# A vision-transformer block on one core: attention folded by query position, second norms split over two engines, FFN order and outputs rearranged

## The chip, the cores and the metric

One core of one Trainium2 chip runs the whole program. The metric is the device time of one execution in microseconds (us); lower is better. The kernel before takes 272.5 us (median of 3 runs, 272.32 to 272.61). Engines are named as in the profile: PE is TensorE (PEld its weight loads), DVE is VectorE, ACT is ScalarE, POOL is GpSimd, SP is SyncE, which here only issues transfers.

## The reference, cut to what matters

32 images of 128x128 become 64 patch tokens each, plus one class token; the width is 128 channels. Then one attention layer and one layer of experts, each behind a layer norm:

```python
h = tok(x)                                     # (32, 64, 128), gated noisy linears, + positions
h = concat([cls_tok, h], axis=1)               # (32, 65, 128)
# attention, 8 heads of 16 channels, relative positions in keys and values
attn1 = einsum('bhqd,bhkd->bhqk', rq, rk)
attn2 = einsum('bhqd,qkd->bhqk', rq, rel_k[idx])
attn = softmax((attn1 + attn2) / sqrt(c), axis=-1)
w1 = einsum('bhqk,bhkd->bhqd', attn, rv)
w2 = einsum('bhqk,qkd->bhqd', attn, rel_v[idx])
h = h + (w1 + w2) @ Wo + bo                    # input: layernorm(h)
# experts on xf = layernorm(h)
probs = softmax(xf @ Wr.T + br); comb = the two largest of 8, the rest 0
o_e = gelu(xf @ W1[e] + b1[e]) @ W2[e] + b2[e]     # hidden width 256
h = h + sum_e comb[:, e] * o_e
```

## The kernel before, in words

Everything stays in SBUF in float32. The 2048 patch tokens are 16 tiles of 128 (one tile is a pair of images, 2 x 64 positions); the 32 class tokens are a 17th, small tile. Four tiles are a block of 512 tokens (`BLK`). Every engine runs a program of its own, written out by hand in order; `S[...]` are semaphores, so an instruction that waits holds all that stands behind it on its engine.

Stages: tokens and first norm (to about 45 us), relative-key scores (to 69 us), the loop over 16 pairs of images (to about 117 us), relative values, projection and second norm (to 148 us), experts (to the end).

The pair loop. PE turns scores (`turn_scores`, L1201), makes the next pair's (`scores`), turns probabilities (`turn_probs`, L1221) and multiplies them with values (`values`). DVE takes the maxima (L744, L751), writes the difference for the class key (L756), the reciprocal of the sum (L762), adds the relative scores for the next pair (`add`, L728), copies the turned probabilities out (`probs`, L769) and, every second pair, the products (`outputs`, L819). ACT does 8 exponentials of 64 columns per pair (L496). POOL scales the probabilities (L351). After the loop DVE spreads the class-key probabilities (`repeat`, L825), PE turns them (L1249), DVE multiplies and adds them (`class_key`, L836 and L841). Meanwhile POOL forms the low part of the first expert weights (`w1_lo`, L355), after ACT has made the high part.

Relative values: for each query position q one matrix of relative values goes against `PT` (the turned probabilities), 4 column groups per q, 256 matmuls, into banks 4 to 7 (`region_c,RVBD` in the rows). DVE adds them with the value bias (L883) to `OT`, which is laid out image by image. Only then does the projection with Wo run, its tiles again pairs of images. The residual is added by DVE for blocks 0 and 1 (L901), by PE through an identity product for blocks 2 and 3. Moments (L633, L636), the power -0.5 on POOL (L367), normalising on DVE (L648), turning on PE (`turn2`, L1325), two evacuations on ACT (L509, L510), and `low` (the part that the high-precision format leaves over; POOL for blocks 0, 1, DVE for the rest, L928) lead to the experts.

Experts: `up(e, blk)` is 6 matmuls of 416 columns (three products of high and low parts, twice), ACT's gelu follows (L518), `down(e, g)` multiplies with W2, DVE accumulates with the routing weight (L992). `up(0, *)` runs between the turns, then `up(1, *)`; two `down` groups of expert 0 come ahead of the routing weights' turn (L1401). At the end SP issues nine output transfers (L280, L283).

`keep_warm(n)` is n products of the identity whose result nobody reads.

## Time and profile before

| what | us |
|---|---|
| median of 3 runs | 272.5 |
| profiled execution, whole | 271.41 |
| its span (first to last instruction) | 269.6 |
| PE busy | 240.5 (89%) |
| DVE busy | 163.9 (61%) |
| ACT busy | 129.5 (48%) |
| POOL busy | 60.3 (22%) |

The granted clock of TensorE is 9 tenths or more in all 40 slices, 1.000 on average (its higher level, 2.4 GHz). A busy engine is not always the one that decides: the share is an average over stages. In the rows, times are from the start of the span; the bracket at the end of a row is the idle time before it and what ended it.

### The profile page before, as it was taken

The numbers are of one execution on the slowest core, as the hardware profiler recorded it, in microseconds if no ns is written. First come the engines' busy times: TensorE is split into PE (matmuls) and PEld (weight loads), VectorE is DVE, ScalarE is ACT, GpSimd is POOL, SyncE is SP. The second block draws the span as 40 slices with busy tenths as digits, with TensorE's granted clock in tenths as the row PEclk, the third lists the DMA queues.
The fourth block names the chain that finished last, engine by engine and source line by source line (L and its number), as shares of the span: only waits on it lengthen the run. The fifth ranks groups of instructions, "written<-read, shape, count | busy, mean of one in ns | idle before, by whom it ended". The sixth has DMA issues, their size and how long they took to land.

```text
span 269.6 us, 6432 instructions
## 1 busy us (share of the span) xinstructions
PE 240.5 (89%) x2519; PEld 206.7 (77%) x2519; DVE 163.9 (61%) x512; ACT 129.5 (48%) x432; POOL 60.3 (22%) x77
## 2 busy tenths in 40 slices
PE   0999997999896788897599989999999999999993
PEld 0855564898774565676479988899999999999993
DVE  0576898635579999999779655535252525252453
ACT  1543047942397999980004886440707071717100
POOL 8930122292013535365015300000000000000000
PEclk9999999999999999999999999999999999999999
DMA  6960000000000000090000000000000000000015
GB/s 214 284 151 2 1 0 0 2 4 0 2 0 4 2 2 2 25 291 5 2 5 0 0 4 0 2 0 2 0 0 1 2 0 2 0 4 0 0 29 131
DMA packets 6554, 7.95 MB, mean 29 GB/s; under 512 B 833, under 2 KB 5295, under 8 KB 6396
## 3 DMA queue, kind: packets, MB, share of 16 engines
q1 hardware_dynamic: 5260, 6.32, 8.3%
q10 hardware_dynamic: 720, 0.87, 1.2%
q8 instruction: 20, 0.33, 0.5%
q0 software_dynamic: 544, 0.35, 0.5%
q14 instruction: 10, 0.08, 0.1%
HBM read 6.47 MB, written 1.06 MB: 28 GB/s over the span
## 4 chain that ended last, share of the span: by engine, by line
PE 61%; DVE 24%; DMA 4%; issue 3%; ACT 3%; POOL 2%; SPq 1%; DVEq 0%
PE banks L1002 55%; DMA region_a<-in_x 4%; DVE stb L728 3%; DVE top L744 3%; DVE stb L648 2%; DVE stats L633 2%; DVE xnT L841 2%; PE banks L1201 2%; DVE region_c L769 2%; ACT region_d L518 2%; POOL rstd L317 2%; DVE mv L636 1%; DVE h L624 1%; DVE ntop L751 1%; SPq L259 1%
## 5 line engine op out<-in xcount | busy, mean ns | idle before, releaser
L992 DVE SCALAR_TENSOR_TENSOR KT<-banks,vbd,KT 128x128 f32<-128x128 f32 (+1 forms) x136 | 38.1, 343 | 59.1 <-PE banks L1002 59.1
L518 ACT ACTIVATE region_d<-banks,vecs 128x416 f32<-128x416 f32 x80 | 45.5, 612 | 47.7 <-PE banks L1002 47.6
L1002 PE MATMUL banks<-w_all,region_d 128*128 128x128 f32 (+1 forms) x544 | 63.3, 276 | 0.0
L1002 PEld LDWEIGHTS banks<-w_all,region_d 128*128 128x128 f32 (+1 forms) x544 | 61.3, 187 | 1.6 <-issue 0.5
L496 ACT ACTIVATE region_e<-banks,ntop 128x64 f32<-128x64 f32 x128 | 38.2, 325 | 6.9 <-DVE rsum L762 3.5
L1002 PE MATMUL banks<-x_hi,w_hi 128*128 128x416 f32 x80 | 29.7, 371 | 1.3 <-ACT region_d L518 1.3
L1002 PE MATMUL banks<-x_lo,w_hi 128*128 128x416 f32 x80 | 28.2, 353 | 0.0
L1002 PE MATMUL banks<-x_hi,w_lo 128*128 128x416 f32 x80 | 28.2, 352 | 0.0
L496 ACT ACTIVATION_READ_ACCUMULATOR region_e<-banks,ntop 128x1 f32 x128 | 27.8, 217 | 0.0
L351 POOL TENSOR_TENSOR region_e<-region_e,rsum 128x512 f32<-128x512 f32 (+1 forms) x16 | 16.5, 1030 | 37.3 <-DVE rsum L762 37.3
L1002 PEld LDWEIGHTS banks<-x_hi,w_hi 128*128 128x128 f32 x80 | 15.1, 189 | 3.5 <-ACT region_d L518 2.0
L1201 PE MATMUL banks<-kc,stb 128*128 128x128 f32 x64 | 10.3, 284 | 7.6 <-DVE stb L728 7.6
L1002 PE MATMUL banks<-kc 128*128 128x128 f32 x70 | 10.2, 292 | 6.6 <-DMA kc<-in_consts 6.6
L1002 PE MATMUL banks<-region_d,relk_bd 64*128 64x64 f32 x256 | 15.3, 288 | 0.0
L1002 PEld LDWEIGHTS banks<-x_lo,w_hi 128*128 128x128 f32 x80 | 15.0, 188 | 0.2
L1002 PEld LDWEIGHTS banks<-x_hi,w_lo 128*128 128x128 f32 x80 | 15.0, 188 | 0.2
L1002 PEld LDWEIGHTS banks<-region_d,relk_bd 64*128 64x128 f32 x256 | 14.6, 188 | 0.6 <-issue 0.5
L1002 PE MATMUL banks<-region_b,wnT 128*128 128x512 f32 x32 | 14.7, 598 | 0.2 <-DVE region_b L566 0.2
L1201 PEld LDWEIGHTS banks<-kc,stb 128*128 128x128 f32 x64 | 6.8, 141 | 9.9 <-DVE stb L728 9.9
L1002 PEld LDWEIGHTS banks<-kc 128*128 128x128 f32 x70 | 9.0, 202 | 6.8 <-DMA kc<-in_consts 6.6
L1002 PE MATMUL banks<-region_c,RVBD 128*32 128x32 f32 x520 | 9.3, 240 | 5.0 <-issue 3.7
L1002 PEld LDWEIGHTS banks<-region_c,RVBD 128*32 128x32 f32 x520 | 8.3, 127 | 5.7 <-issue 4.2
(219 smaller groups left out, 379.3 us busy)
## 6 DMA issues: line engine op xcount, KB each, us to landing
region_a<-in_x SPq DMA_DIRECT2D x2, 512.0 KB, 6.3
region_a<-in_x SPq DMA_DIRECT2D x1, 1024.0 KB, 10.3
w_sb<-in_L_ffn_W SPq DMA_DIRECT2D x1, 1024.0 KB, 5.9
out<-KT SPq DMA_DIRECT2D x8, 128.0 KB, 2.4
region_d<-in_L_attn_rel_v SPq DMA_DIRECT2D x2, 260.0 KB, 9.2
kc<-in_consts ACTq DMA_DIRECT2D x1, 336.0 KB, 5.8
region_d<-in_L_tok_eps_in ACTq DMA_DIRECT2D x2, 128.0 KB, 7.5
region_d<-in_L_tok_W_w ACTq DMA_DIRECT2D x1, 128.0 KB, 7.2
```

What stands on the lines that cost most here:

```text
L317: g.tensor_tensor(rstd[:, n * TPB:(n + 1) * TPB], ve[:, n * TPB:(n + 1) * TPB], mhalf[:, :], ALU.pow).then_inc(S["rstd_ok"], 1)
L351: g.tensor_tensor(ev, ev, rv, ALU.mult).then_inc(S["pn_ok"], 1)
L496: last = a.activation(dst[:, h // 2, h % 2], src[:, h // 2, h % 2], ACT.Exp, scale=SCALE, bias=ntop[:, o + h:o + h + 1], accum_out=esum[:, ...
L518: a.activation(HB[:, e % 2, s, blk * FB:(blk + 1) * FB], bank[h_bank(i)][:, 0:FB], ACT.Gelu, bias=vecs[:, v:v + 1]).then_inc(S["gelu_ok"], 1)
L633: last = v.bn_stats(stats[0:m, 6 * t:6 * t + 6], src[0:m, t * C:(t + 1) * C])
L648: last = v.tensor_scalar(ST[n % 2][0:m, i * C:(i + 1) * C], src[0:m, t * C:(t + 1) * C], mv[0:m, 2 * t:2 * t + 1], rstd[0:m, t:t + 1], ALU ...
L728: v.tensor_tensor(ST[p % 2].rearrange("p (g j m) -> p g j m", g=2, j=2), banks[:, 0:1024].rearrange("p (g h j m) -> p g h j m", g=2, h=2, ...
L744: most = mark(v.tensor_reduce(top[:, o].rearrange("p (j s) -> p j s", j=PJ), bank[2 + p % 2][:, :].rearrange("p (j k s) -> p j s k", j=PJ, ...
L769: v.tensor_copy(PT[:, :, 2 * p:2 * p + 2, 0:NPATCH], bank[4 + p % 2][:, :].rearrange("p (j b q) -> p j b q", j=PJ, b=2)).then_inc(S["pt_ok ...
L992: last = v.scalar_tensor_tensor(acc[0:m, t, :], bank[out_bank(u)][0:m, i * C:(i + 1) * C], comb[0:m, t, e:e + 1], acc[0:m, t, :], op0=ALU. ...
L1002: return t_.matmul(o, l, r, start=start, stop=stop)
L1201: last = t_.transpose(bank[2 + p % 2][:, j * P:(j + 1) * P], ST[p % 2][:, j * P:(j + 1) * P], ident)
```

## The change

The parts, in the order of the program:

1. Class scores (`class_products`) are computed as four 32-row groups instead of full 128-row products padded with zeros.
2. In the loop, POOL writes the class-key difference (`difference`) and spreads the class-key probabilities (`repeat`), two pairs at a time; PE turns them in the loop (`turn_pc`), DVE multiplies them in the loop (`class_key`, 256 columns), and `outputs` adds them and the value bias while it copies.
3. `OT` is laid out by query position: column = 32 q + image. A tile of 128 columns is now four query positions of 32 images. So a block of 16 positions can be projected once its relative values are there. The residual `h0` must have the same layout: SP writes it to the output tensor in HBM in the old layout and reads it back in the new one, during the loop.
4. The relative values are cut into halves of a block, with the projections and the first turn between them, and one identity product (`keep_warm(1)`) behind every four positions of the first six quarters.
5. The residual is DVE's in all four blocks; the second norm of blocks 0 to 2 is ACT's (`norm2`, with a factor and an offset `nmr` = -mean x rstd that DVE and POOL prepare), of the rest DVE's; `low` is DVE's throughout.
6. `up(0, blk)` and `up(1, blk)` alternate; gelu number i belongs to `UNITS[i]`. Four `down` groups of expert 0 (`AHEAD = 4`, before 2) come ahead of the routing weights' turn.
7. The last expert takes the class tile first and tiles 12 to 15 in two halves (`LAST`); the outputs are issued by SP and ACT.

```diff
+LAST = [range(16, 17), range(0, 4), range(4, 8), range(8, 12), range(12, 14), range(14, 16)]
+AHEAD = 4
-OP_BANKS = (5, 6, 2, 3)
+OP_BANKS = (1, 2, 3, 5)
+REL_BANKS = (4, 5, 6, 0)
+        OTq = OT[:, :].rearrange("p (q b) -> p q b", b=IMG)
+        UNITS = [(e, blk, s) for blk in range(5) for e in range(2) for s in range(2)]
+        UNITS += [(e, blk, s) for e in range(2, E) for blk in range(5) for s in range(2)]
...
 # SP, during the pair loop
+            sp_.wait_ge(S["h0o_ok"], 1)
+            sp_.wait_ge(S["st_ok"], 5)
+            for b2 in range(2):
+                sp_.dma_start(ov[b2, 1:QC, :, :], h0v[64 * b2:64 * b2 + 64, :, :]).then_inc(S["d_h0s"], 16)
+            sp_.wait_ge(S["d_h0s"], 32)
+            sp_.wait_ge(S["st_ok"], 10)
+            for f in range(4):
+                sp_.dma_start(h0v[32 * f:32 * f + 32, :, :], oq[f]).then_inc(S["d_h0q"], 16)
...
 # POOL, pair loop
+            for p in range(PAIRS + 2):
+                if p < PAIRS:
+                    difference(p)
+                if p >= 2:
+                    normalised(p - 2)
+                    if p % 2 == 1:
+                        repeat((p - 3) // 2)
...
 # ACT
-            for n in (2, 3):
-                act.wait_ge(S["op_ps"], n + 1)
-                a.activation(KT[:, n * BLK:(n + 1) * BLK], bank[OP_BANKS[n]][:, :], ACT.Copy).then_inc(S["h1a_ok"], 1)
+            def norm2(n):
+                act.wait_ge(S["nmr_ok"], n + 1)
...
+                    last = a.activation(ST[n % 2][0:m, i * C:(i + 1) * C], KT[0:m, t * C:(t + 1) * C], ACT.Identity,
+                                        bias=nmr[0:m, t:t + 1], scale=rstd[0:m, t:t + 1])
...
 # DVE, pair loop: outputs and class key
-                v.tensor_copy(OT[:, 256 * u:256 * u + 256].rearrange("p (b q) -> p b q", b=4), o[:, :, 0:NPATCH])
+                dve.wait_ge(S["pcx_ok"], u + 1)
+                v.scalar_tensor_tensor(OTq[:, :, 4 * u:4 * u + 4].rearrange("p q b -> p b q"), o[:, :, 0:NPATCH],
+                                       vecs[:, V_BV:V_BV + 1], own(u), op0=ALU.add, op1=ALU.add)
...
 # DVE, behind the loop
+            attended(0)
+            attended(1)
+            residual(0)
+            attended(2)
+            residual(1)
+            attended(3)
+            low(0)
+            attended_class()
+            residual(2)
+            low(1)
+            residual(3)
...
+            low(2)
+            norm2(3)
+            norm2(4)
...
 # PE, behind the loop
-            for n in range(1, 5):
-                turn2(n)
-                router(n - 1)
...
-                up(0, n - 1)
+            filled(0, range(16))
+            filled(1, early)
+            project(0)
+            relative(1, late)
+            relative(2, early)
+            project(1)
+            relative(2, late)
+            relative(3, early)
+            project(2)
+            turn2(0)
+            relative(3, late)
+            relative_class()
...
+            project(3)
...
+            up(0, 0)
+            turn2(1)
+            router(0)
+            up(1, 0)
+            up(0, 1)
+            turn2(2)
...
```

How the rows move, at three places. First DVE in the pair loop, an odd pair from its maxima on; before:

```order
L744 TENSOR_REDUCE top<-banks 128x8
L751 SCALAR_TENSOR_TENSOR ntop<-top,nSc 128x8
L756 TENSOR_TENSOR region_e<-ntop,nSc 128x8
L762 RECIPROCAL rsum<-esum 128x8
L728 TENSOR_TENSOR stb<-banks,region_a 128x512
L769 COPY region_c<-banks 128x4x2x64
L819 COPY xnT<-banks 128x256
L820 COPY OTc<-banks 128x4
L740 TENSOR_TENSOR esum<-esum,region_e 128x8
```

and the same stretch after (`xnT` is the memory of `OT`, `region_c` that of `PT`):

```order
L824 TENSOR_REDUCE top<-banks 128x8
L832 SCALAR_TENSOR_TENSOR ntop<-top,nSc 128x8
L838 RECIPROCAL rsum<-esum 128x8
L914 TENSOR_TENSOR tmpx<-banks,vcq 128x256
L808 TENSOR_TENSOR stb<-banks,region_a 128x512
L849 COPY region_c<-banks 128x4x2x64
L900 SCALAR_TENSOR_TENSOR xnT<-banks,vecs,tmpx 128x4x64
L902 COPY OTc<-banks 128x4
L820 TENSOR_TENSOR esum<-esum,region_e 128x8
```

The small difference (L756) has left DVE, the class-key product (L914) has come in, and the copy has become an addition.

Second, PE from the last values on (`RVBD` relative values, `wqkvo` the projection, `kc` alone a fill, `stb` a turned norm); before:

```order
L1002 MATMUL banks<-region_c,vbd 32x65 x8
L1002 MATMUL banks<-region_c,RVBD 32x32 x256
L1002 MATMUL banks<-p0x,kc 128x32
L1002 MATMUL banks<-region_c,RVBD 32x32 x4
L1002 MATMUL banks<-h,kc 128x512
L1002 MATMUL banks<-wqkvo,xnT 128x128 x8
L1002 MATMUL banks<-wqkvo,OTc 32x128
L1002 MATMUL banks<-wqkvo,xnT 128x128 x4
L1002 MATMUL banks<-h,kc 128x512
L1002 MATMUL banks<-wqkvo,xnT 128x128 x4
L1002 MATMUL banks<-kc 128x128 x9
L1325 MATMUL banks<-kc,stb 128x128 x4
```

and after, from the sixth quarter of the relative values on:

```order
L1075 MATMUL banks<-region_c,RVBD 32x32 x16
L1075 MATMUL banks<-kc 128x128
L1075 MATMUL banks<-wqkvo,xnT 128x128 x4
L1075 MATMUL banks<-region_c,RVBD 32x32 x64
L1075 MATMUL banks<-wqkvo,xnT 128x128 x4
L1075 MATMUL banks<-region_c,RVBD 32x32 x64
L1075 MATMUL banks<-wqkvo,xnT 128x128 x4
L1396 MATMUL banks<-kc,stb 128x128 x4
L1075 MATMUL banks<-region_c,RVBD 32x32 x32
L1075 MATMUL banks<-p0x,kc 128x32
L1075 MATMUL banks<-region_c,RVBD 32x32 x4
L1075 MATMUL banks<-kc 128x128 x2
```

Three of four projections and the first turn now stand between the relative values, and the two products with `h` are gone.

Third, DVE behind the loop; before:

```order
L883 SCALAR_TENSOR_TENSOR xnT<-banks,vecs,xnT 128x32x16 x4
L886 SCALAR_TENSOR_TENSOR OTc<-banks,vecs,OTc 128x32
L888 SCALAR_TENSOR_TENSOR OTc<-banks,clsv,OTc 128x32
L891 TENSOR_TENSOR clsr<-clsr,bob 32x128
L892 MEMSET lg 128x8
L893 MEMSET vbd 128x640
L901 TENSOR_TENSOR KT<-banks,h 128x512
L633 BN_STATS stats<-KT 128x6 x4
L636 BN_AGGR mv<-stats 128x2 x4
L638 TENSOR_SCALAR ve<-mv 128x4
```

and after:

```order
L945 TENSOR_TENSOR xnT<-banks,xnT 128x512 x2
L960 TENSOR_TENSOR KT<-banks,h 128x512
L710 BN_STATS stats<-KT 128x6 x4
L713 BN_AGGR mv<-stats 128x2 x4
L717 TENSOR_SCALAR nmr<-mv 128x4
L719 TENSOR_SCALAR ve<-mv 128x4
L945 TENSOR_TENSOR xnT<-banks,xnT 128x512
L960 TENSOR_TENSOR KT<-banks,h 128x512
```

The first residual stands behind two blocks of relative values instead of four, and the next blocks follow in turns.

## Rows read from the trace of the kernel before

**Rows 1.** Busy time by stretch: length, engines (busy, count), clock, DMA share, GB/s.

```profile
core 0: us, PE busy (x) PEld busy (x) DVE busy (x) ACT busy (x) POOL busy (x), PEclk, DMA share, GB/s
121.80:136.30 14.50, 9.49 (x536) 8.59 (x525) 11.30 (x15) 0.00 (x0) 3.38 (x1) 1.00 0.02 5
136.30:147.80 11.50, 11.17 (x91) 9.72 (x84) 10.56 (x54) 2.90 (x6) 4.33 (x4) 1.00 0.01 1
147.80:165.30 17.50, 16.20 (x98) 14.93 (x98) 10.60 (x36) 15.11 (x29) 2.92 (x3) 1.00 0.01 1
165.30:265.30 100.00, 99.99 (x764) 95.66 (x762) 39.93 (x138) 36.51 (x65) 0.00 (x0) 1.00 0.03 6
```

**Rows 2.** Timeline of PE: start, length, instruction; idle time before it in brackets.

```profile
113.97 1.38 PE L1002 MATMUL banks<-kc 128*128 128x128 f32 x10
...
122.85 2.14 PE L1002 MATMUL banks<-region_c,RVBD 128*32 128x32 f32 x128 [0.46 <-issue]
126.30 1.77 PE L1002 MATMUL banks<-region_c,RVBD 128*32 128x32 f32 x103 [1.31 <-issue]
...
134.03 1.77 PE L1002 MATMUL banks<-region_c,RVBD 128*32 128x32 f32 x103 [1.58 <-issue]
...
137.27 1.95 PE L1002 MATMUL banks<-wqkvo,xnT 128*128 128x128 f32 x16
...
146.51 0.63 PE L1325 MATMUL banks<-kc,stb 128*128 128x128 f32 x4 [0.33 <-DVE stb L648]
...
147.80 0.46 PE L1002 MATMUL banks<-x_hi,w_hi 128*128 128x416 f32 x1
```

**Rows 3.** Timeline of DVE, one even and one odd pair of the loop.

```profile
90.47 0.67 DVE L728 TENSOR_TENSOR stb<-banks,region_a 128x512 f32<-128x512 f32 x1
...
92.62 0.17 DVE L751 SCALAR_TENSOR_TENSOR ntop<-top,nSc 128x8 f32<-128x8 f32 x1
92.82 0.17 DVE L756 TENSOR_TENSOR region_e<-ntop,nSc 128x8 f32<-128x8 f32 x1
92.91 0.20 DVE L762 RECIPROCAL rsum<-esum 128x8 f32<-128x8 f32 x1
93.02 0.67 DVE L728 TENSOR_TENSOR stb<-banks,region_a 128x512 f32<-128x512 f32 x1
...
95.79 0.67 DVE L728 TENSOR_TENSOR stb<-banks,region_a 128x512 f32<-128x512 f32 x1
```

**Rows 4.** The page's costliest groups, two of ACT: busy, mean ns, idle, releaser.

```profile
L518 ACT ACTIVATE region_d<-banks,vecs 128x416 f32<-128x416 f32 x80 | 45.5, 612 | 47.7 <-PE banks L1002 47.6
...
L496 ACT ACTIVATE region_e<-banks,ntop 128x64 f32<-128x64 f32 x128 | 38.2, 325 | 6.9 <-DVE rsum L762 3.5
```

**Rows 5.** Timeline of PE at the loop's start, class scores.

```profile
71.91 1.60 PE L1002 MATMUL banks<-KT,wnT 128*128 128x128 f32 x12
```

**Rows 6.** Timeline of DVE behind the loop.

```profile
120.69 0.68 DVE L836 TENSOR_TENSOR tmpx<-banks,vcq 128x512 f32<-128x512 f32 x1
121.40 4.32 DVE L841 TENSOR_TENSOR xnT<-xnT,tmpx 128x512 f32<-128x512 f32 x1
...
138.46 0.69 DVE L901 TENSOR_TENSOR KT<-banks,h 128x512 f32<-128x512 f32 x1 [0.29 <-PE banks L1002]
...
141.49 0.87 DVE L633 BATCH_NORM_STATS2 stats<-KT 128x6 f32<-128x128 f32 x4
142.40 0.38 DVE L636 BATCH_NORM_AGGREGATE mv<-stats 128x2 f32<-128x6 f32 x4
```

**Rows 7.** Timeline of POOL behind the loop.

```profile
120.39 4.79 POOL L355 TENSOR_TENSOR w_lo<-w_sb,w_hi 128x2048 fp32r<-128x2048 f32 x1 [1.33 <-ACT w_hi L504]
...
143.06 1.04 POOL L367 TENSOR_TENSOR rstd<-ve,mhalf 128x4 f32<-128x4 f32 x1 [1.28 <-DVE ve L638]
```

**Rows 8.** Timeline of SP at the end.

```profile
267.23 0.61 SPq L283 DMA_DIRECT2D out<-KT  x1
```

**Rows 9.** The page's DMA issues: KB each, us from issue to landing.

```profile
out<-KT SPq DMA_DIRECT2D x8, 128.0 KB, 2.4
...
out<-KT SPq DMA_DIRECT2D x1, 16.0 KB, 2.0
```

433 lines of the change are left out of this document (236 added, 197 removed).

## The prediction

> **What bounds the kernel now.** I read the busy time by stretch first. From 165.3 to 265.3 us PE is busy 99.99 of 100 us, and from 147.8 to 165.3 it works 16.20 of 17.50 [rows 1]: the experts are PE's own work, and a change of order saves there at most the 1.3 us of gaps. Between 121.8 and 136.3 PE is busy 9.49 of 14.50 us, and from 136.3 to 147.8 it seems busy (11.17 of 11.50), but only until the first `up` at 147.80 [rows 1, 2], with 15 `keep_warm` products and two identity products of the residual among the rest. So of the 26 us between the last values (121.8) and the first `up` much is waiting or fill. The timeline of PE shows what kind: after every 128 product records (64 matmuls) of relative values it stops "on issue", 1.31 and 1.58 us; two blocks of 128 records start 126.30 - 122.85 = 3.45 us apart, and another pair 1.58 + 2.14 = 3.72 apart, while the work is 2.14 [rows 2]. It looks as if the code itself arrives at such a rate: 128 records each 3.45 to 3.72 us. The second wait is DVE's: L841 stands 4.32 us where another 512-column addition (L901) takes 0.69, and it ends soon after POOL's `w1_lo` (120.39 + 4.79 = 125.18) [rows 6, 7]. And residual, moments, power, normalising and turning follow one another only after all relative values. In the pair loop DVE is the pace: 2.55 us for an even pair, 2.77 for an odd one (starts of L728) [rows 3]; ACT is idle only 6.9 us in the whole loop [rows 4].
>
> **The change part by part.** Times below are those of the profiled execution (span 269.6, whole 271.41); the median of the runs is 272.5, 1.1 above it, and I add this again at the end.
>
> Class scores. 12 records take 1.60 us [rows 5] for 6 products, three such portions; in four column groups 32 rows each run side by side, so 16 products of 32 rows should take half. PE then no longer holds DVE in the first three pairs. Bounds: 0 (DVE's and ACT's own work hides it) and 2.4 us (three portions shortened by half of 1.60); DVE's and ACT's work lies close behind PE's there, so I take 1.0 gained, somewhat under the middle.
>
> The loop. DVE loses L756: from L751 to L762 pass 0.29 us now, 0.1 of them needed, so 0.2 is saved per pair [rows 3]. An odd pair gains `class_key`, 256 columns: between the 0.17 of an 8-column and the 0.67 of a 512-column operation [rows 3], 0.42 long, some 0.35 to the next start. `outputs` has two more operands but the same 256 columns: 0. Two pairs: 5.32 - 0.4 + 0.35 = 5.27 against 5.32; ACT's floor is below (it idles 6.9 us in 16 pairs [rows 4]). So per pair nothing changes. Bounds over 8 double pairs: -1.6 (if the copy hid anyway) and +2.4 (if DVE waits 0.3 us per double pair for the two turns that PE now makes in front of the scores). I take 0. POOL gets the difference, and a copy of 256 columns every second pair, some 0.5 to 0.9 us each; its share of the loop is under half now, so that is hidden; what it costs without cover is the rival D below.
>
> Behind the loop. The four 512-column copies of DVE (`repeat`) and six of its eight class-key operations, among them the one of 4.32 us, are no longer there. But PE still runs 5 + 3 fills (1.38 us for 5 [rows 2]), the last turns wait for ACT's last pair and POOL, and DVE has the last class key between. Followed, the last values end at about 119.8 instead of 121.8: 2.0 earlier (1.0 from the start of the loop, 1.0 here). Bounds 0.5 and 3.5.
>
> From the relative values to the first `up`. PE's work in the new order: 256 matmuls, 4 x 2.14 = 8.6; four projections at half of 1.95 = 3.8; 8 fills at 0.27 = 2.2; one turn 0.5, the class row and its projection 0.9. Sum 15.9 to 16.0. Records: 512 + 32 + 16 + 16 = 576, that is 4.5 blocks of 128. At 3.72 per block the code needs 16.7, at 3.45 15.5; but blocks whose own work is longer (projections in them) don't lend time to others. Block by block the excess is 0.8, 0.4, 0.75, 0.35 at 3.72, sum 2.3; at 3.45 it is 1.3. I take 2.3, and 0.3 for small waits on data: 18.5. The first `up` starts at 119.8 + 18.5 = 138.3 instead of 147.8: 9.5 earlier.
>
> Do data arrive in that time? DVE: relative block 1 is complete on PE at about 128.0, `attended(1)` 0.7, then residual 0.69, moments 0.87 + 0.1 + 0.38, two small ones, to 131.0 [rows 6]; POOL's power 1.04 [rows 7] and a small product to 132.5; ACT's four of 128 columns, each between the 0.325 of 64 and the 0.612 of 416 columns [rows 4], about 1.1, to 133.8. PE wants the first turn at about 133.8 as well: a draw, so a wait here is likely to be small, and each later one similarly: `low(0)` ends at 137.2, before `up(0, 0)`. Queued behind `residual(0)` on DVE is `attended(2)` (project(2) waits for it), behind each `norm2` on ACT the gelus and evacuations. From the first `up` PE has about 3.9 us per block (two `up`, one turn, one router), and per block DVE needs 2.3 + 0.7, ACT 1.1 + 1.2 + 2.4 = 4.7 at first, later less, since DVE norms the last blocks: ACT is the tight one, but PE runs some banks ahead. I cost that at 0, bounds 0 and 4.
>
> Experts. `turn2(1)` and `router(0)` were ahead of the first `up` and are now behind it: 147.80 - 146.51 = +1.3 [rows 2]. The gaps of 1.3 us between 147.8 and 165.3 [rows 1] should go: four `down` groups (7 us of PE work) now stand between the router and the turn of the routing weights, while the two table loads and DVE's selection run; by hand comb is ready at 160.4 and PE comes to its turn at 163.2. So -1.3. Bounds: -1.3 and +1.5.
>
> The end. 4.3 us pass from PE's last product to the end (265.3 to the span of 269.6) [rows 1]: DVE's accumulation, SP's last issue at 267.23, 2.0 us landing [rows 8, 9]. After: two tiles instead of four plus one in DVE's last turn (saves some 0.5), but two issues of 0.61 in each queue behind one another and 2.4 for the larger ones [rows 8, 9]. I take 0; bounds -1.0 and +0.5.
>
> HBM round trip of `h0`: eight quarter-megabytes in and out during the loop, where the queues are empty; it is wanted at about 128.7 and issued before 96. It has more than 30 us for 16 times what lands in 2.4 [rows 9]. Cost 0; without that cover the first residual would wait for it.
>
> Sum: -9.5 + 1.3 - 1.3 + 0 = -9.5. Profiled execution 271.4 - 9.5 = 261.9; median 272.5 - 9.5 = 263.0.
>
> **Two rules weighed.** On code: the trace shows the stops of 1.31 and 1.58 us per 128 records [rows 2]. The Trainium skill, "Runtime: NRT & Kernel Launch", section "Instruction fetch mechanics", says that code comes in blocks of 256 instructions and that crossing a block's edge is mostly hidden. A block of 256 is 128 products with their weight loads, so the spacing agrees; "mostly hidden" does not here. By the page the stretch would take 2.3 less, 260.7 in all.
>
> B, the hand-overs hold PE: ACT (norm, two evacuations, gelus) or the in-order DVE queue is late at turns 0 to 3. For it speaks the draw at 133.8 and ACT's 4.7 against 3.9 per block; against it, that PE has banks to run ahead. Price: 0.8 per block for four blocks and a first turn 1 us late, +4: 267.
> C, it goes better: fills cover the code stops (2.3) or the loop ends earlier: 260.5. For it: a fill takes only 2 records for 0.27 us, so blocks are longer; against it: they still fall short of 3.72.
> D, slower: one mechanism, DVE's two-SBUF operations in the loop (L740, L751) waiting behind POOL's longer turn. If each pair met one whole POOL operation (1.04, the size of the power operation in [rows 7]; L351 is as long), 14 pairs cost 14.6: 263.0 + 14.6 = 277.6. It decides from 9.5 / 14 = 0.68 us a pair. Against it: POOL's turn begins with the reciprocal and DVE's next two operations read PSUM, so that only the end of the spreading copy can meet L740, some 0.2 us.
> E, nothing of the early `up` remains because the projection by query position needs all relative values anyway (it doesn't do what it says): 272. Against it: the tile's columns are four positions of all images, and its wait is for one block.
>
> **How the numbers follow.** A 0.55 (its own range 261 to 265.5), B 0.24, C 0.16, D 0.03, E 0.02. The range 259.5 to 268 leaves out the far part of C, and of B, and D and E, together under 0.2. Within 0.2% (0.5 us) is about what a measurement of this kernel can tell from no change. Faster 0.95, same 0.02, slower 0.03.
>
> **What would show it.** Right: the first 416-column product at about 138, turn 0 waiting under 1 us, PE without a gap over 0.5 from there to its end at about 256, no DVE operation of 4 us, L914 in 0.42 and double pairs of 5.3. Wrong: PE waiting for `stb` or for x_lo by more than 1 us per block (B), `issue` stops gone (C), L820 or L832 over 0.5 us in the loop (D), project(0) waiting for the last relative block (E). Should the granted clock fall from its higher level (2.4 GHz, all stretches of [rows 1] show it) in the new order, all sums of PE are off.

## The result and the profile after

The changed kernel takes 261.57 us (median of 4 runs, 260.73 to 262.57), the kernel before beside it 272.41 (272.25 to 272.61): ratio 0.960, 95% interval 0.956 to 0.964, faster. The forecast was 263.0. The profiled execution took 261.36 us, 10.1 less than the 271.41 of before; its span is 259.5.

The page's busy time and clock. PE is busy 91% of a shorter span, and no slice has a granted clock under 0.9 of full speed, that is the higher level, 2.4 GHz:

```profile
PE 236.2 (91%) x2507; PEld 202.2 (78%) x2507; DVE 153.7 (59%) x485; ACT 132.5 (51%) x442; POOL 64.4 (25%) x104
...
PEclk9999999999999999999999999999999999999999
```

Busy time by stretch, against [rows 1]:

```profile
120.00:137.00 17.00, 16.43 (x581) 14.05 (x578) 8.42 (x32) 3.25 (x8) 6.94 (x5) 1.00 0.03 6
137.00:155.00 18.00, 18.00 (x116) 16.43 (x116) 11.57 (x45) 15.79 (x32) 3.23 (x4) 1.00 0.00 1
155.00:255.00 100.00, 100.00 (x765) 96.31 (x765) 43.50 (x152) 39.05 (x69) 0.00 (x0) 1.00 0.02 6
```

From 120 to 137 PE works 16.43 of 17.00 us, where it worked 9.49 of 14.50 in the stretch of the relative values before; from 137 on it has no gap. The timeline of PE there, against [rows 2]:

```profile
120.13 0.66 PE L1075 MATMUL banks<-region_c,RVBD 128*32 128x32 f32 x32
120.72 0.49 PE L1075 MATMUL banks<-kc 128*128 128x128 f32 x2
121.14 0.67 PE L1075 MATMUL banks<-region_c,RVBD 128*32 128x32 f32 x32
...
126.14 1.06 PE L1075 MATMUL banks<-wqkvo,xnT 128*128 128x128 f32 x8
127.13 2.15 PE L1075 MATMUL banks<-region_c,RVBD 128*32 128x32 f32 x128
...
131.73 1.39 PE L1075 MATMUL banks<-region_c,RVBD 128*32 128x32 f32 x76 [0.42 <-issue]
...
134.36 0.66 PE L1396 MATMUL banks<-kc,stb 128*128 128x128 f32 x4
...
138.47 0.46 PE L1075 MATMUL banks<-x_hi,w_hi 128*128 128x416 f32 x1
```

The last values end and relative values begin at 120.13 (121.80 before); the first `up` starts at 138.47 (147.80). Projections (`wqkvo`) and the turn of block 0 (L1396) lie between relative values, and one stop on issue is left, 0.42 us, where there were 0.46, 1.31 and 1.58 [rows 2]. A group of 32 records comes every 1.02 us with its fill (120.13, 121.14), and 128 without fills take 2.15, so 32 take 0.54: a fill costs 0.48.

The chain that feeds the turn, on DVE, POOL and ACT. DVE's operation of 4.32 us [rows 6] is gone:

```profile
128.35 0.69 DVE L945 TENSOR_TENSOR xnT<-banks,xnT 128x512 f32<-128x512 f32 x1 [3.68 <-PE banks L1075]
128.96 0.68 DVE L960 TENSOR_TENSOR KT<-banks,h 128x512 f32<-128x512 f32 x1
...
131.32 1.02 POOL L411 TENSOR_TENSOR rstd<-ve,mhalf 128x4 f32<-128x4 f32 x1 [6.83 <-DVE ve L719]
...
132.66 1.65 ACT L574 ACTIVATE stb<-KT,nmr,rstd 128x128 f32<-128x128 f32 x4 [12.80 <-POOL nmr L415]
```

The chain starts when PE ends block 1 of the relative values (L945 waits for it). It ends at 134.31, and PE takes the turn at 134.36. The draw that the prediction saw at 133.8 looks like one here; the run below tells which side ends last.

One double pair of the loop on DVE, against [rows 3]; from one L808 to the next but one is 97.79 - 92.36 = 5.43 us (5.32 before):

```profile
92.04 0.40 DVE L914 TENSOR_TENSOR tmpx<-banks,vcq 128x256 f32<-128x256 f32 x1
92.36 0.68 DVE L808 TENSOR_TENSOR stb<-banks,region_a 128x512 f32<-128x512 f32 x1
...
93.55 0.65 DVE L900 SCALAR_TENSOR_TENSOR xnT<-banks,vecs,tmpx 128x256 f32<-128x256 f32 x1
94.05 0.16 DVE L902 COPY OTc<-banks 128x4 f32<-128x4 f32 x1
...
94.89 0.17 DVE L832 SCALAR_TENSOR_TENSOR ntop<-top,nSc 128x8 f32<-128x8 f32 x1
94.98 0.20 DVE L838 RECIPROCAL rsum<-esum 128x8 f32<-128x8 f32 x1
...
97.79 0.68 DVE L808 TENSOR_TENSOR stb<-banks,region_a 128x512 f32<-128x512 f32 x1
```

The experts: the routing weights (L1036) are there at 159.46, and PE comes to their turn (L1507) at 163.11 without idling:

```profile
159.16 0.30 DVE L1036 TENSOR_TENSOR vbd<-rt 128x136 f32<-128x136 f32 x1
...
163.11 0.60 PE L1507 MATMUL banks<-kc,vbd 128*128 128x128 f32 x4
```

The end, against [rows 8]; the last product ends at 249.80 + 5.86 = 255.66 us, 3.84 before the span does:

```profile
249.80 5.86 PE L1075 MATMUL banks<-w_all,region_d 128*128 128x128 f32 x51
...
251.50 6.27 SPq L304 DMA_DIRECT2D out<-KT  x10
251.50 6.37 ACTq L614 DMA_DIRECT2D out<-KT  x10
```

**A ruler for all runs.** The pair loop's first maximum (L824, L744 before) starts anywhere from 71.5 to 72.9 us in these executions. So each profiled execution is cut at that start, the first relative value, the first 416-column `up` and the last product's end, all read off the timelines:

| kernel | loop | relative values to first `up` | `up` to PE's end | tail | median, us |
|---|---|---|---|---|---|
| before | 50.28 | 26.00 | 117.49 | 4.31 | 272.4 |
| after | 48.08 | 18.34 | 117.19 | 3.84 | 261.6 |
| after_again | 48.72 | 18.34 | 117.19 | 3.89 | 262.1 |
| e1_relative_first | 48.09 | 25.25 | 117.95 | 3.88 | 269.9 |
| e2_no_fills | 48.08 | 17.80 | 117.19 | 3.93 | 261.3 |
| e3_two_ahead | 48.04 | 18.36 | 117.71 | 3.86 | 262.1 |
| e4_one_queue | 48.07 | 18.34 | 117.18 | 6.87 | 265.0 |
| e5_dve_norms | 48.06 | 19.11 | 118.04 | 3.96 | 263.5 |
| e6_no_loop_fills | 48.07 | 19.73 | 117.18 | 3.87 | 262.9 |
| e7_rows_of_four | 48.67 | 18.34 | 117.19 | 3.87 | 262.8 |
| e8_dc_on_dve | 51.54 | 18.36 | 117.16 | 3.90 | 265.3 |
| e10_contiguous | 47.56 | 18.35 | 117.18 | 3.92 | 260.8 |
| e12_both | 48.04 | 16.81 | 117.20 | 10.55 | 267.2 |
| e13_images_first | 47.56 | 17.16 | 117.17 | 3.92 | 260.3 |

Where an edit doesn't touch a stretch, it repeats to 0.05 us nearly everywhere (the tail to 0.12), so an edit is read from its own stretch far better than from the medians, whose intervals are about 0.3 to 0.5% (0.8 to 1.3 us). The loop of after_again is an outlier; the granted clock was 0.89 from 69 to 84 us, around its start (1.00 in the first profile). So the 10.1 us are: loop -2.20, relative stretch -7.66, experts -0.30, tail -0.47, and +0.53 for a later start of the loop in that execution. The stretches of before and after don't hold quite the same work: before, the turn and the routing product of the next block (146.51 to 147.80, 1.3 us [rows 2]) stand ahead of the first `up`; after, they stand behind it. Like for like the relative stretch is about 6.4 shorter and the experts about 1.6.

### The profile page after: what moved, and what is told of

It is laid out like the page before. It is cut to its first block, busy times and chain, and to the rows that moved or that the text cites. A ratio compares the mean times of both kernels' runs of the same rounds, so it can differ in the third digit from the quotient of the medians.

```text
span 259.5 us, 6469 instructions
## 1 busy us (share of the span) xinstructions
PE 236.2 (91%) x2507; PEld 202.2 (78%) x2507; DVE 153.7 (59%) x485; ACT 132.5 (51%) x442; POOL 64.4 (25%) x104
## 3 DMA queue, kind: packets, MB, share of 16 engines
q10 hardware_dynamic: 1952, 1.41, 1.9%
## 4 chain that ended last, share of the span: by engine, by line
PE 63%; DVE 17%; issue 6%; ACT 4%; POOL 4%; DMA 4%; ACTq 1%; DVEq 0%; POOLq 0%
PE banks L1075 58%; DMA region_d<-in_L_tok_W_sw 4%; DVE top L824 4%; DVE stb L808 3%; POOL w_lo L405 2%; ACT region_e L541 2%; PE banks L1276 2%; POOL rstd L338 2%; DVE stb L728 2%; DVE region_c L849 2%; DVE stats L710 1%; DVE h L701 1%; PE banks L1396 1%; ACT w_hi L549 1%; PE banks L1085 1%
## 5 line engine op out<-in xcount | busy, mean ns | idle before, releaser
L541 ACT ACTIVATION_READ_ACCUMULATOR region_e<-banks,ntop 128x1 f32 x128 | 31.8, 255 | 0.0
L1075 PE MATMUL banks<-region_d,relk_bd 64*128 64x64 f32 x256 | 15.3, 288 | 0.0
L1075 PEld LDWEIGHTS banks<-kc 128*128 128x128 f32 x56 | 8.0, 208 | 7.4 <-DMA kc<-in_consts 6.5
L824 DVE TENSOR_REDUCE top<-banks 128x8 f32<-128x512 f32 x16 | 11.0, 687 | 1.9 <-PE banks L1276 1.4
L1075 PE MATMUL banks<-region_d,region_b 64*128 64x128 f32 x128 | 11.4, 297 | 0.3 <-ACT region_a L517 0.3
```

Source lines behind the costliest of these rows:

```text
L541: last = a.activation(dst[:, h // 2, h % 2], src[:, h // 2, h % 2], ACT.Exp, scale=SCALE, bias=ntop[:, o + h:o + h + 1], accum_out=esum[:, ...
L824: most = mark(v.tensor_reduce(top[:, o].rearrange("p (j s) -> p j s", j=PJ), bank[2 + p % 2][:, :].rearrange("p (j k s) -> p j s k", j=PJ, ...
L1075: return t_.matmul(o, l, r, start=start, stop=stop)
```

## The experiments

**after_again**, the changed kernel once more.

> The changed kernel itself, as the mark for the three runs beside it, which differ from it by less than 1 us each. Expected: 261.6 us, within 0.3% of its own first result, and the same marks in the trace within 0.1 us: last values ended about 120.1, first 416-column up product at 138.5, last product at 255.7.

262.07 us (ratio 0.961, 0.956 to 0.966). Its marks lie 0.65 us later, all from the loop, and here the draw at turn 0 went the other way:

```profile
135.00 0.66 PE L1396 MATMUL banks<-kc,stb 128*128 128x128 f32 x4 [0.67 <-ACT stb L574]
```

PE waits 0.67 us for ACT, but it had no stop on issue ahead of that, and the stretch is 18.34 us again. The turn comes 14.22 us after the first relative value here and 14.23 in the first profile. So do those of e3, e4, e7 and e10 (14.23 or 14.24), where PE waits 0.51 to 0.84 us for ACT. What ends last at turn 0 is therefore the chain over DVE, POOL and ACT, in the first profile too; its stop of 0.42 us on issue cost nothing.

**e1_relative_first**, the order alone.

```diff
             filled(1, early)
-            project(0)
             relative(1, late)
-            relative(2, early)
-            project(1)
-            relative(2, late)
-            relative(3, early)
-            project(2)
-            turn2(0)
-            relative(3, late)
+            relative(2, range(16))
+            relative(3, range(16))
+            pe.wait_ge(S["o_ok"], 1)
             relative_class()
+            project(0)
+            project(1)
+            project(2)
+            turn2(0)
```

> Edit: TensorE's order behind the loop. The changed kernel runs the projections 0 to 2 and the turn of block 0 between the relative values of the next positions; here all 512 records of relative values and the class ones come first, then projections 0, 1, 2 and the turn; fills, layout and all the rest stay. Theory: the gain of 9.3 us ahead of the first up product comes from this order, since the chain from a projection to its turned block (residual, norm, POOL's power, ScalarE, turn: 5.2 us from 128.96 to 134.36 by VectorE's L960 to L1396) then runs beside relative values. Without it the projection of block 0 comes at about 134.5 instead of 126.1, its residual at 137.4, turn 0 at 142.8, and the first up product, behind block 0's evacuations and its neighbours' columns, at about 144 to 146: 267 to 268 us, +6 us against the changed kernel. Rival: the order only fills gaps in the delivery of TensorE's code (the run without the six fills showed that 6 x 0.48 us of fills hid in it, all but 0.5 us of it), so that the records take as long and the later chain costs 2 us or less: 264. Either way the relative stretch itself would show issue stops again between 127 and 134, because nothing lies between the records there: 3 blocks of 128 records at 3.1 to 3.9 us.

269.93 us (ratio 0.990, 0.987 to 0.993); the stretch is 25.25 us, 6.9 longer, nearly the 26.00 of before. Without the interleaving the stretch is 0.75 us under that of before, which holds 1.3 us more work; the order brings the rest. (The wait on `o_ok` keeps the class values out of a bank that DVE still reads; it is met by then.) The timeline of PE:

```profile
131.65 2.13 PE L1075 MATMUL banks<-region_c,RVBD 128*32 128x32 f32 x124 [1.30 <-issue]
...
135.10 0.30 PE L1075 MATMUL banks<-region_c,RVBD 128*32 128x32 f32 x6 [0.77 <-issue]
135.33 2.05 PE L1075 MATMUL banks<-wqkvo,xnT 128*128 128x128 f32 x16
139.53 1.16 PE L1075 MATMUL banks<-wqkvo,xnT 128*128 128x128 f32 x8 [2.15 <-DVE xnT L945]
142.00 1.11 PE L1396 MATMUL banks<-kc,stb 128*128 128x128 f32 x4 [1.31 <-ACT stb L574]
...
143.76 1.92 PE L1075 MATMUL banks<-wqkvo,xnT 128*128 128x128 f32 x8
```

and its busy time with the granted clock (0.51) just behind:

```profile
142.00:148.00 6.00, 6.00 (x24) 5.34 (x24) 3.45 (x15) 2.99 (x7) 1.21 (x3) 0.51 0.00 0
```

The expected stops come back, PE waits 3.46 us for data, and then something that I had not expected: behind these waits the granted clock is at its lower level (1.2 GHz), and the turn takes 1.11 us instead of 0.66, eight projection records 1.92 instead of 1.06. From the turn to the first `up` pass 4.17 us, where the same products take 2.45 in the changed kernel (134.36 to 134.94 and 136.60 to 138.47); so an estimate from these rows puts 1.7 of the 6.9 us down to the clock. The first `up` came at 146.17, just past the 144 to 146 expected.

**e2_no_fills**.

```diff
                 for i in range(part[0], part[-1] + 1, 4):
                     relative(n, range(i, i + 4))
-                    keep_warm(1, spare=3)
```

> Edit: the six 128-column filling products between the first six groups of relative values are taken out; nothing else. Theory of the fills: in the changed kernel a group of 32 records with its fill takes 1.02 us and 32 records of an unfilled run take 0.54 us (128 in 2.15), so a fill costs 0.48 us, not the 0.27 that I forecast; six are 2.9 us, and without them TensorE is at the first projection 2.9 us earlier. The first up product would then come up to 2.9 us earlier (135.6) unless VectorE's chain from the values to the residuals or the gelu side is late, which I expect to eat about half: total 260.0 (-1.5 us against the changed kernel). Rival, the code: the kernel before delivered 128 of these records per 3.72 us with 'issue' stops of 1.3 to 1.6 us; 192 unfilled records in a row would need 5.6 us, only 0.5 us less than the 6.1 us that they take with fills, the stops come back in the chain or the timeline, and the time is within 0.5 us of the changed kernel's. A third outcome, slower by over 1 us, would mean that the fills hold TensorE's granted clock up: then the clock of the stretch 120 to 137 would fall below 0.9.

261.28 us (ratio 0.957, 0.952 to 0.962). The stretch is 0.54 us shorter, for 2.9 us of work less:

```profile
120.98 2.39 PE L1075 MATMUL banks<-region_c,RVBD 128*32 128x32 f32 x144
124.09 0.91 PE L1075 MATMUL banks<-region_c,RVBD 128*32 128x32 f32 x48 [0.72 <-issue]
...
127.99 1.04 PE L1075 MATMUL banks<-region_c,RVBD 128*32 128x32 f32 x56 [0.67 <-issue]
...
131.99 1.17 PE L1075 MATMUL banks<-region_c,RVBD 128*32 128x32 f32 x64 [0.78 <-issue]
...
135.99 0.42 PE L1075 MATMUL banks<-region_c,RVBD 128*32 128x32 f32 x12 [0.36 <-issue]
```

2.53 us of stops come back. The records behind them start at 124.09, 127.99, 131.99 and 135.99, and between two of these starts there are each time exactly 128 records (48 + 72, 56 + 64 and 64 + 52 relative ones, the rest a projection or a projection and a turn): a block of code every 3.9 to 4.0 us. The rival holds: most of the fills stood where PE would have waited for its code. The clock stayed at 1.00. How much comes back is not the same in every execution, and the profiled one is the slowest of six (259.10 to 261.75 us). e12 and e13, further down, have the same order of products without fills, and their blocks arrive sooner: e13's start 3.62 and 3.73 us apart (122.83, 126.45, 130.18), and e12 passes two of them in 7.08 us.

The rows of e13:

```profile
122.83 0.91 PE L1077 MATMUL banks<-region_c,RVBD 128*32 128x32 f32 x48 [0.91 <-issue]
...
126.45 1.04 PE L1077 MATMUL banks<-region_c,RVBD 128*32 128x32 f32 x56 [0.41 <-issue]
```

So their stretches are 17.16 (e13) and 16.81 us (e12), and the fills are worth 0.5 to 1.5 us. Why the blocks arrive at different rates is open.

**e6_no_loop_fills**.

```diff
-                if PAIRS <= p < PAIRS + 2:
-                    if p == PAIRS:
-                        pe.wait_ge(S["pcx_ok"], 5)
-                    keep_warm(5 if p == PAIRS else 3, spare=0)
```

> Edit: the two blocks of filling products (five and three) that TensorE runs in the last two steps of the attention loop are taken out. In the changed kernel they lie at 113.72 (1.38 us) and 115.99 (0.94 us), ahead of the transposes of the last probabilities (115.03 and 116.76), and VectorE's last product waits for the second one until 117.18. Theory: they lie on the path, the last values end 0.5 to 0.8 us earlier (119.4 instead of 120.1), and so do the first up product and the end: 261.0. Rival: ScalarE's last exponentials (end 116.6) are what ends last there, TensorE just waits for them: 0.0 to -0.2 us. Second rival: TensorE's granted clock falls behind the loop without them (below 0.9 in 118 to 130), and the kernel is slower by 1 us or more.

262.93 us (ratio 0.964, 0.960 to 0.968), and nothing that I expected came as a whole:

```profile
115.83 0.66 PE L1298 MATMUL banks<-kc,region_e 128*128 128x128 f32 x4 [1.24 <-POOL region_e L384]
...
120.92 0.67 PE L1075 MATMUL banks<-region_c,RVBD 128*32 128x32 f32 x32
123.01 0.38 PE L1075 MATMUL banks<-kc 128*128 128x128 f32 x2 [1.41 <-issue]
```

In the fills' place PE waits for POOL's normalised probabilities, and the loop keeps its 48.07 us: the first rival was right that the fills cost nothing there, though it is POOL that ends last and not ACT. But a stop of 1.41 us appears behind the first 32 records of relative values, and the stretch grows by 1.39: the stop lies ahead of the chain to turn 0, where PE waits 0.81 us for ACT as well. Products taken out at one place moved a stop to another, where nothing covered it; whether by shifting the blocks' edges or by the time that PE gave the delivery, no run separates.

**e7_rows_of_four** and **e10_contiguous**, the mis-sized term. e10 leaves out the order of positions, so it isn't a replacement for the changed kernel. L900 writes with a stride (after), in runs of four with strided reads (e7), or contiguously (e10):

```diff
-  v.scalar_tensor_tensor(OTq[:, :, 4 * u:4 * u + 4].rearrange("p q b -> p b q"), o[:, :, 0:NPATCH],
-                         vecs[:, V_BV:V_BV + 1], own(u), op0=ALU.add, op1=ALU.add)
+e7  v.scalar_tensor_tensor(OTq[:, :, 4 * u:4 * u + 4], o[:, :, 0:NPATCH].rearrange("p b q -> p q b"),
+                           vecs[:, V_BV:V_BV + 1], own(u).rearrange("p b q -> p q b"), op0=..., op1=...)
+e10 v.scalar_tensor_tensor(OT[:, 256 * u:256 * u + 256].rearrange("p (b q) -> p b q", b=4),
+                           o[:, :, 0:NPATCH], vecs[:, V_BV:V_BV + 1], own(u), op0=..., op1=...)
```

> Edit: VectorE's addition of the own values (one 256-column scalar_tensor_tensor in each second pair of the loop) writes its result position by position, in contiguous runs of four elements, and reads PSUM and the own values with the stride instead; the same elements, the same place. In the changed kernel the operation is 0.65 us long and holds VectorE for 0.50 us to its next start; the same operation with contiguous writes took 0.33 before. Theory: the strided write is the 0.16 us per double pair that I had costed at nothing; turned to runs of four it goes back to 0.33 to 0.40, a double pair from 5.43 to 5.30, the loop ends 0.8 to 1.3 us earlier and so does the kernel: 260.5. Rival: a stride costs the same on either side (read or write), the operation stays at 0.50 and the time does not move (within 0.2 us); or it is worse, since two inputs are strided now: +0.1 us per double pair, +0.8 us.

> Edit: the 256-column addition of the own values writes its result contiguously, image by image, as the copy that it replaced did (L819 before: 0.41 us, 0.33 us to the next start). The output projection then reads the positions in another order than the rest of the kernel keeps them in, so the tokens of the result are permuted against the reference; no time hangs on the values. In the changed kernel it is 0.66 us with a strided write and was 0.65 us with strided reads instead. Theory: any stride beyond one element costs, on either side; contiguous, the operation falls to 0.42 us, a double pair from 5.43 to 5.27, the loop ends 1.2 us earlier: 260.6. Rival: it is the operation itself that is dear (three inputs: PSUM, a per-partition scalar and the own values), it stays at 0.65 us, and the time is that of the changed kernel. That would put my mis-sized term on the added operand and not on the new order of positions.

262.77 us (ratio 0.965) and 260.84 us (0.957, 0.954 to 0.960). L900 in the groups of e7 and of e10 (busy, mean ns, idle):

```profile
L900 DVE SCALAR_TENSOR_TENSOR xnT<-banks,vecs,tmpx 128x256 f32<-128x256 f32 x5 | 3.2, 649 | 0.0
```

```profile
L900 DVE SCALAR_TENSOR_TENSOR xnT<-banks,vecs,tmpx 128x256 f32<-128x256 f32 x4 | 1.9, 475 | 0.0
```

About 655 ns with strided writes, 649 with strided reads, 475 contiguous; the plain copy before took 414. Of the 0.24 us that the operation grew, 0.18 belong to the stride, on whichever side, and 0.06 to the two added operands. The loop became 0.52 us shorter, under half of what I expected, since a double pair fell by only 0.10 (5.34). What counts is the time to DVE's next start: 0.33 us for the copy (94.21 to 94.54), 0.50 after (93.55 to 94.05), 0.39 in e10 (94.27 to 94.66). The stride has 0.11 of these 0.17 us. In e7 it is 0.57 (94.32 to 94.89) at the same length, and a double pair is 5.51 (93.13 to 98.64): eight times 0.08 are the 0.6 us by which e7's loop is longer. The Trainium skill, "SBUF — State Buffer", section "Door 1: The DMA port swizzle", says that each access that crosses to a new 16-byte line of SBUF pays a penalty. The trace agrees in kind: strides of 128 bytes on the write (after) and of 256 on the SBUF read (e7) cost 0.18 us here, and runs of four elements on the write side did not help, since the reads then stride.

**e8_dc_on_dve**.

```diff
-                        dve.wait_ge(S["dc_ok"], p - 1)
+                    dve.wait_ge(S["top_ok"], p + 1)
+                    if p >= 4:
+                        dve.wait_ge(S["pc_ok"], p - 3)
+                    v.tensor_tensor(SP[p % 4][:, 512:520], ntop[:, o], nSc[:, p * H:(p + 1) * H], ALU.subtract)
```

> Edit: the subtraction that gives the class-key difference of a pair (128x8) goes from POOL back to VectorE, where the kernel before had it (its L756), right behind ntop; 16 of them. Theory: in the kernel before it took VectorE 0.09 us to the next start (92.82 to 92.91) and waited for ntop; VectorE is busy in all of the loop, so a double pair goes from 5.43 to 5.6 us and the loop ends 1.4 us later: 263.2. My prediction had counted 0.18 us a double pair for this move. Rival: POOL's hand-over (0.20 us of POOL, then ScalarE's exponentials behind it) is shorter when VectorE does it itself, ScalarE starts a pair earlier, and nothing is lost: 261.8, within 0.3 us. If POOL's shared path with VectorE mattered, VectorE's short operations L820 and L832 (0.15 and 0.17 us now) would get shorter without it; I expect them unchanged.

265.31 us (ratio 0.972, 0.969 to 0.976), more than either expectation. The expectation misstates the prediction's term, which was 0.4 a double pair, and that is what the timeline shows: 0.28 us from L829 to L840 against 0.09 from L832 to L838.

```profile
93.68 0.17 DVE L829 SCALAR_TENSOR_TENSOR ntop<-top,nSc 128x8 f32<-128x8 f32 x1
93.88 0.17 DVE L834 TENSOR_TENSOR region_e<-ntop,nSc 128x8 f32<-128x8 f32 x1
93.96 0.20 DVE L840 RECIPROCAL rsum<-esum 128x8 f32<-128x8 f32 x1
```

The loop is 3.46 us longer, and 16 x 0.19 = 3.0 of it is this. So this small move carries more than the whole gain of the loop: without it the loop would be 1.3 us longer than before.

**e3_two_ahead**: `AHEAD = 2`, with `down(0, 2)` and `down(0, 3)` behind the first `base`.

> Edit: two groups of down products ahead of TensorE's turn of the routing weights instead of four (the number that bounds the buffer goes from 4 to 2, the two others follow behind base(0)). In the changed kernel the routing weights (comb) are ready at 159.46 and TensorE comes to them at 163.11. Two down groups are about 2 x 1.55 us of TensorE, so it would come at about 160.0, still 0.5 us behind their being ready. Theory, as I now read the trace: +0.0 to +0.5 us. My prediction put 1.3 us on this edit of the change (gaps ahead of the routing weights that go); if that holds, the time is 1.3 us longer and an idle time ahead of L1507 shows. Rival: with fewer groups ahead, ScalarE's gelus of the next blocks fall behind TensorE and up products wait for buffers: more than +1.5 us.

262.07 us (ratio 0.961, 0.958 to 0.964). The stretch from the first `up` is 0.52 us longer: the upper end of what I expected, under half of the prediction's 1.3. The turn of the routing weights (L1504) comes at 160.44, right behind DVE's last step of the selection (L1036, 160.00 to 160.30), where the changed kernel leaves 3.65 us between:

```profile
160.44 0.63 PE L1504 MATMUL banks<-kc,vbd 128*128 128x128 f32 x4
```

**e4_one_queue**: ScalarE's ten block transfers and the class row's go to SyncE.

> Edit: all 21 output transfers are issued by SyncE's queue; ScalarE's queue issues none. In the changed kernel each queue issues half, 0.43 to 0.45 us each, and the execution ends 3.84 us behind the last product. The last group (tiles 14 and 15) has four transfers: in one queue its fourth is issued 2 x 0.43 us later. Theory: the tail is 0.9 us longer (4.7 us), +0.3% in all, with 262.5 us against 261.6; if the earlier groups' issues are not done by the time the last values come, a little more, up to +1.7. Rival: the landing of the transfers, not their issue, ends the execution, and the tail is unchanged within 0.2 us.

265.04 us (ratio 0.973, 0.970 to 0.975): a tail of 6.87 us, 3.0 longer, three times my figure.

```profile
252.27 9.47 SPq L306 DMA_DIRECT2D out<-KT  x20
```

All twenty issues of the blocks stand in one row from 252.27 to 261.74. The first of them starts 4.16 us before PE's end (256.43), and in that time one queue issues nine at 0.47. I had counted only the last group.

**e5_dve_norms**: second norm of blocks 0 to 2 by DVE.

> Edit: the second norm of blocks 0 to 2 goes from ScalarE (four activations, 1.65 us, behind a product of mean and deviation on VectorE and POOL) to VectorE, as blocks 3 and 4 have it in the changed kernel; only the power stays on POOL. In the first two profiles of the changed kernel turn 0 started at 134.36 (no wait) and 135.00 (0.67 us wait for ScalarE's L574): data and TensorE arrive within 0.7 us of each other. Theory: VectorE does a block's norm in about 1.2 to 1.7 us plus the hand-over, but it has in hand the next residual (0.68) and its statistics, so turn 0 moves by -0.3 to +0.5, and the turns 1 to 3 come later because VectorE (11.6 us busy of the 18 from 137 on) gets about 4 us more work there. TensorE's up products wait for x_lo by 0.5 to 2 us: 262.5 to 263.5. Rival: VectorE has room, the norms hide, and what ScalarE saves (4.95 us) brings the gelus and nothing else forward: within 0.3 us of the changed kernel.

263.50 us (ratio 0.967, 0.965 to 0.970), at the far end of the expected range: 0.77 us in the relative stretch and 0.85 behind it. The row of PE at the class row's projection:

```profile
139.66 0.41 PE L1068 MATMUL banks<-wqkvo,OTc 128*32 128x128 f32 x2 [1.35 <-DVE OTc L942]
```

The norms' price is what queues behind them on DVE: here the class row, for whose projection PE waits, and behind it on PE the first `up`.

**e12_both**: e2, the last group split in two, and one transfer per tile.

```diff
-                for f in range(2):
-                    sp_.dma_start(oq[f][:, tt, :], acc[32 * f:32 * f + 32, tt, :])
+                for t in (t for t in tiles if t % 2 == 0):
+                    sp_.dma_start(ot[t], acc[:, t, :])      # ot: "b (t f) c -> t f b c"
```

> A version meant to beat both. Edits: the six fills between the first relative values taken out (0.5 to 0.8 us in their own run); one output transfer per token tile of all 128 partitions, even tiles by SyncE and odd ones by ScalarE, 17 issues of 64 KB in place of 21 of 32 or 64 KB; and the last expert's last group of two tiles split in two of one tile. Expected: behind the last value there is one VectorE operation (0.28) instead of two, one issue per queue (0.45) instead of two, then the landing (1.8 us): tail 3.84 to 3.1 us; with the fills' 0.5 the time is 260.4 us, -1.2 against the changed kernel. Rival: a transfer that reads 128 partitions of 512 bytes is no quicker to land than two of 32 partitions and two tiles, or the landing grows with the issues in flight (e4: one queue, tail 6.9 us): tail unchanged, 261.2.

267.19 us (ratio 0.981, 0.977 to 0.984): a tail of 10.55 us, 6.6 longer instead of 0.7 shorter. The DMA share (tenths) and GB/s in 40 slices of 250 to 266, first e12, then the changed kernel in 250 to 260:

```profile
DMA  0000122222222222222222222222222222220000
GB/s 0 0 0 0 23 79 74 84 76 82 77 87 79 87 85 86 81 82 78 86 87 87 87 85 87 86 87 86 87 87 86 86 86 87 86 77 4 0 0 0
```

```profile
DMA  2000000004899800489980028999945647200000
GB/s 60 2 0 4 0 0 0 0 0 96 150 312 230 250 12 0 92 141 314 236 250 16 0 63 150 285 250 299 250 125 152 158 105 185 78 0 0 0 0 0
```

The transfers run at 86 GB/s with a share of 0.2 to 0.3, a quarter of the sixteen engines, against up to 314 GB/s and nine tenths. The Trainium skill, "DMA: Bandwidth & Descriptors", section "Why a DMA increments its semaphore by 16 and not by 1", has the number of engines chosen by the outermost dimension of both patterns; mine was 4 in HBM, 32 in the changed kernel, and the trace agrees. The issues also changed in number and partitions, and no run changed this dimension alone. Its relative stretch (16.81) has the order of e2, with two stops (1.11 and 0.51 us) for e2's four.

**e13_images_first**: e2's edit; L900 contiguous; the position order made behind the loop by the four additions.

```diff
-                o = OT[:, n * BLK:(n + 1) * BLK]
-                v.tensor_tensor(o, bank[REL_BANKS[n]][:, :], o, ALU.add)
+                v.tensor_tensor(OTp[:, n * BLK:(n + 1) * BLK].rearrange("p (q b) -> p q b", b=IMG),
+                                bank[REL_BANKS[n]][:, :].rearrange("p (q b) -> p q b", b=IMG),
+                                OTq[:, 16 * n:16 * n + 16, :], ALU.add)
```

> A version meant to beat both, with the full result. Edits: the six fills between the first relative values are taken out, and the order of positions is no longer made in the loop: VectorE's addition of the own values writes contiguously, image by image (0.475 us in the run of the contiguous write, against 0.655), and the four 512-column additions of the relative values behind the loop (L945) read the attended values with the stride and write the position order into the free place of the probabilities, from which the projection reads. Expected from the two single runs: the loop 0.5 us shorter (a double pair 5.43 to 5.335), the fills 0.5 to 1.5 us, together 260.3 us, -1.5 against the changed kernel (pooled 261.8). The four additions have a strided input now; two inputs at 512 columns already take 0.69 us, so I expect 0.69 to 1.05 each, and 0.4 us at most of it ahead of turn 0, hidden behind relative values: 0. Rival: turn 0 is already the last to come without fills (TensorE there at 133.3 to 134.1), the stride costs 0.36 us on the chain to it, and half of the gain goes again: 261.0. Second rival: VectorE's stride by 64 elements collides with something and the additions take 2 us: slower than 262.

260.33 us (ratio 0.957, 0.954 to 0.960), the best version: loop -0.52, relative stretch -1.18 against the changed kernel's first profile. The additions take 1.03 to 1.06 us instead of 0.69, hidden as expected:

```profile
125.99 1.06 DVE L945 TENSOR_TENSOR region_e<-banks,xnT 128x512 f32<-128x512 f32 x1 [3.14 <-PE banks L1077]
```

The changed kernel's medians are 261.57 and 262.07, so this is 1.2 to 1.7 less, but the ratios' intervals overlap (0.954 to 0.960 against 0.956 to 0.964). The loop's -0.52 is as in e10. Of the -1.18, e2's and e12's 17.80 and 16.81 tell that up to 1 us depends on how fast the code arrived in the execution.

## Why the prediction was right, and where not

The forecast was 261.9 for the profiled execution and 261.36 came. For the median it was 263.0, and 261.57 came: it added 1.1 us for the distance of median and profile, which is 0.2 here. Term by term:

- Start of the loop, class scores: 1.0. From the first maximum to the sixth, 15.3 us before (71.52 to 86.81) and 13.9 after (72.05 to 85.92): 1.4. Right in kind; the new form alone was not run. The forecast had no term for the loop's later start, 0.5.
- The loop, "`outputs` has two more operands but the same 256 columns: 0". This is the step that failed: L900 takes 0.65 for 0.41, that is 0.17 more a double pair to its next start, and the double pair is 5.43 for the forecast 5.27. From the sixth maximum to the last ntop are 27.6 us, 27.1 before: 0.5 longer for the forecast 0. e10 shows that the stride of the new order is most of it (0.11). The term beside it, 0.4 from the difference moved to POOL, is right (e8).
- Behind the loop: 1.0 forecast; from ntop's last at 113.90 to the relative values at 121.80 were 7.9 us, now 113.53 to 120.13, 6.6: 1.3. With the rest the relative values start at 120.13 for the forecast 119.8.
- To the first `up`: 18.5 forecast, 18.34 twice. The sum is right, two of its terms are not, and that they cancel is in part luck: the eight fills cost 0.48 each, not 0.27 (1.7 us more), and the stops on issue 0.42 or 0, not 2.3. That PE's code bounds the stretch is not what the changed kernel shows, since turn 0 waits for the chain that ends on ACT (0.51 to 0.84 us in after_again, e3, e4, e6, e7, e8 and e10); without fills it is (e2, e12, e13), at 3.5 to 4.0 us per 128 records for the 3.45 to 3.72 assumed. Rival C's sign, stops on issue gone, is there, but the fills' own price took most of its 2.3 us.
- The data's draw at turn 0: 134.31 against 134.36, or a wait of 0.67; the data are last by a little. ACT's normalising took 1.65 us, not 1.1: four instructions of 128 columns cost 0.41 each.
- Why -9.5 comes from the order: e1 gives 7.7 us back, 6.9 in the stretch and 0.8 behind it. The lower clock is about 1.7 of the first (estimate above) and all of the second: the first five `up` products take 1.83 us there (146.17 to 148.00) and 1.05 in the changed kernel (138.47 to 139.52).
- Experts: +1.3 and -1.3 forecast, -0.30 in sum measured, so some 1.6 gained for 1.3. e3 gives 0.5 of the 1.3 for two of the four `down` groups; the rest was not taken apart.
- The end: 0 forecast, -0.47 measured. It rests on the second queue, to which the sum gave no price of its own: without it +3.0 (e4).
- Rival D, DVE behind POOL in the loop: L820 and L832 stay at 0.15 and 0.17 us; not seen. Rival B: not seen, and e5 shows how near it is. Rival E: refuted by project(0) at 126.14, with two and a half blocks of relative values still to come. The round trip of `h0` through HBM cost nothing, as forecast: the last read is issued at 97.3, the slowest of these transfers lands in 6.6 us, and the first residual at 128.96 doesn't wait.

The first of the two rules weighed, "Instruction fetch mechanics" of the Trainium skill's "Runtime: NRT & Kernel Launch", would have made the total 260.7, 0.9 us under the measured median, and the profiled execution 259.6, 1.8 under, and in the changed kernel hardly a stop is seen. But e2 and e6 show that they are hidden by the fills, at a price, and not by themselves.

## What to carry to other kernels

When small products arrive more slowly than TensorE runs them, the stretch is at least as long as its code takes to arrive, and other engines' chains should be started inside it: interleaving the projections brought 7.7 of 10 us, and taking out 2.9 us of fill work brought 0.5 to 1.5. Price an edit in the stretch that it touches, cut at marks in the timeline; totals could not have told 0.5 us from 1.5. Where PE waits for code, one profile can't either, since the arrival differs from run to run. A transfer's outermost dimension and an operation's stride are parts of a layout change's price: 6.6 us of tail, and 0.11 us of DVE's pace an operation here.
